# A graph attention layer on one Trainium2 core: all tiles of edges gathered by indirect DMA

## The reference

```python
Qh = (x @ Wq.T + bq).reshape(n, H, D)          # H = 4 heads of D = 16
Kh = (x @ Wk.T + bk).reshape(n, H, D)
Vh = (x @ Wv.T + bv).reshape(n, H, D)
Ee = (edge_attr @ We.T + be).reshape(-1, H, D)
score = (Kh[src] * Qh[dst] * (1.0 / np.sqrt(D)) * Ee).sum(-1)
score = jnp.exp(jnp.clip(score, -5.0, 5.0))
msg = Vh[src] * score[..., None]
wV = jax.ops.segment_sum(msg, dst, num_segments=n)
x = _layernorm(x + wV.reshape(n, H * D), axis=-1)
```

## Time and profile before

| | us |
|---|---|
| median of three timed runs | 1892.74 (1892.62 to 1893.34) |
| span of the profiled execution | 2801.3 |
| POOL busy in it | 1400.8 (50%) |
| TensorE busy in it | 1925.7 (69%) |
| VectorE busy in it | 1174.3 (42%) |
| ScalarE busy in it | 851.7 (30%) |
| mean granted clock of TensorE, as a share of 2.4 GHz | 0.771 |

### The profile page before, as it was taken

How to read it: one execution, slowest core, us unless ns; L and a number is a source line. 1 busy time by engine, 2 the same in 40 slices (tenths; PEclk the granted TensorE clock), 3 DMA queues, 4 the chain that set the end, 5 groups by cost and what they waited for, 6 DMA issues and landing times. The chain is left out here.

```text
span 2801.3 us, 49920 instructions
## 1 busy us (share of the span) xinstructions
PE 1925.7 (69%) x16647; PEld 1663.0 (59%) x16647; DVE 1174.3 (42%) x2092; ACT 851.7 (30%) x2863; POOL 1400.8 (50%) x1495
## 2 busy tenths in 40 slices
PE   4666677777767667776767676667676667766775
PEld 4555666666656556665656665656565656655665
DVE  4433444444434444444444444434344444434444
ACT  6222222332223223223322222223232223222233
POOL 5444554455554445555445555445545545555443
PEclk7777777777778777787877877778778777778776
DMA  6222222222222222222222222222222222222221
GB/s 194 63 56 57 59 58 58 57 61 57 58 54 59 56 58 60 58 59 59 59 57 58 59 57 58 57 56 60 57 58 58 59 57 60 59 58 59 56 61 45
DMA packets 113024, 171.42 MB, mean 61 GB/s; under 512 B 59952, under 2 KB 60592, under 8 KB 112880
## 3 DMA queue, kind: packets, MB, share of 16 engines
q0 software_dynamic: 46848, 96.04, 13.5%
q1 hardware_dynamic: 66160, 75.18, 9.8%
HBM read 163.85 MB, written 7.23 MB: 61 GB/s over the span
## 5 line engine op out<-in xcount | busy, mean ns | idle before, releaser
L275 POOL DMA_INDIRECT kv<-kv_table,idx x1464 | 1384.4, 946 | 1351.1 <-DVE idx L303 944.9
L675 PE MATMUL xg_bank<-x_parts,src_onehot 128*128 128x192 bf16 x7252 | 904.6, 286 | 102.7 <-issue 99.1
L675 PEld LDWEIGHTS xg_bank<-x_parts,src_onehot 128*128 128x128 bf16 x7252 | 739.8, 115 | 187.4 <-issue 129.2
L803 DVE TENSOR_TENSOR src_onehot<-src_ps,columns 128x1664 bf16<-128x1664 bf16 (+1 forms) x592 | 573.0, 968 | 537.0 <-remote 359.3
L646 PE MATMUL qe_ps<-q_win,onehot_t 128*128 128x128 bf16 x2418 | 250.2, 267 | 407.2 <-issue 389.9
L646 PEld LDWEIGHTS qe_ps<-q_win,onehot_t 128*128 128x128 bf16 x2418 | 194.3, 120 | 441.2 <-issue 439.5
L735 ACT COPY onehot_t<-oht_bank 128x512 bf16<-128x512 bf16 x202 | 118.0, 584 | 1099.3 <-remote 1052.4
L743 ACT ACTIVATE distance<-iota_w,dst_neg 128x64 f32<-128x64 f32 x1612 | 405.9, 337 | 15.4 <-PEq L306 15.4
L656 PE MATMUL sum_ps<-onehot,msg 128*64 128x64 f32 x3224 | 357.7, 290 | 49.3 <-issue 42.4
L656 PEld LDWEIGHTS sum_ps<-onehot,msg 128*64 128x64 f32 x3224 | 319.8, 200 | 111.1 <-issue 93.8
L844 DVE TENSOR_TENSOR msg<-kv,sum_ps 128x512 f32<-128x512 f32 x202 | 138.0, 683 | 563.2 <-ACT sum_ps L772 497.0
(11 more groups left out here) (117 smaller groups left out, 760.9 us busy)
## 6 DMA issues: line engine op xcount, KB each, us to landing
attr_sb<-attr SPq DMA_DIRECT2D x201, 256.0 KB
kv<-kv_table,idx POOLq DMA_INDIRECT x1464
q_win<-q_table SPq DMA_DIRECT2D x404, 24.0 KB
kv_table<-kv_stage SPq DMA_DIRECT2D x7, 448.0 KB, 3.6
q_table<-q_stage SPq DMA_DIRECT2D x7, 336.0 KB
xT_sb<-xT SPq DMA_DIRECT2D x7, 224.0 KB, 4.8
kv_stage<-x_own_rows SPq DMA_DIRECT2D x1, 1568.0 KB
out<-y_sb SPq DMA_DIRECT2D x5, 256.0 KB, 2.0
```

The costliest lines, as they stand in the source:

```text
L275: pool.indirect_dma_start(out=kv[:, slot, t, :], out_offset=None, in_=kv_table, in_offset=bass.IndirectOffsetOnAxis(ap=idx[:, slot, t:t + ...
L675: mm = pe.matmul(xg_ps[k % 2], src_onehot[:, c, :], x_parts[:, c, :, :], start=(c == 0), stop=(c == NT - 1))
L803: dve.tensor_tensor(src_onehot[:, PARTS[part], :], src_ps.unsqueeze(1).to_broadcast([P, n, P]), columns[:, PARTS[part], :], ALU.is_equal). ...
```

## The change

All 1612 tiles are gathered by POOL's indirect DMAs. All that served the 148 tiles on TensorE goes: `x_parts`, `columns`, `src_f`, `minus_first`, `src_seen`, `src_onehot`, `xg_sb`, `xg_t_sb`, the second load of x, nine semaphores of the loop and the schedule. VectorE's wait before line 824 counts eight tiles a turn. The two PSUM banks stay as spare banks for setup and end; the freed PSUM bank of `src_ps` isn't used.

```diff
@@ counts and waits @@
-        def gathered_before(slot, turn):
-            if isinstance(turn, int) and turn == 0:
-                return 0
-            if slot == 2:
-                return turn * T
-            return turn * (T - 1) + (1 if slot < 2 else 0)
-        def pool_tiles(g, slot):
-            return T - 1 if pe_tile(g, slot) else 2 * pairs_of(g)
         def gather(pool, g, slot, first=0, end=T):
-            for t in range(first, min(end, pool_tiles(g, slot))):
+            for t in range(first, min(end, 2 * pairs_of(g))):
                 pool.indirect_dma_start(
...
@@ setup @@
-                sp.dma_start(x_own, x_own_rows).then_inc(x_own_loaded, 16)
                 sp.dma_start(src_sb[:, SLOTS * T:], src_tab[:, SLOTS * T:]).then_inc(src_loaded, 16)
...
-                pool.iota(column_i[:, :], ...).then_inc(column_set, 1)
-                pool.wait_ge(column_set, 1)
-                pool.memset(xg_t_sb[:, :], 1.0).then_inc(consts_zeroed, 1)
-                pool.iota(minus_first_i[:, :], ...).then_inc(iota_set, 1)
...
-                number_columns(HALVES[0])
...
-                act.wait_ge(x_own_loaded, 16)
-                for half in HALVES:
-                    act.copy(x_parts[:, half, 0, :], x_own[:, half, :]).then_inc(x_part0, 1)
-                for n, half in enumerate(HALVES):
-                    act.wait_ge(x_rested, n + 1)
-                    act.copy(x_parts[:, half, 1, :], x_rest[:, half, :]).then_inc(x_part1, 1)
-                act.wait_ge(src_loaded, 32)
-                act.copy(src_f[:, :], src_sb[:, :])
-                number_columns(HALVES[1])
...
-                dve.tensor_copy(minus_first[:, :], minus_first_i[:, :]).then_inc(dst_step, 1)
...
-                for n, half in enumerate(HALVES):
-                    dve.wait_ge(x_part0, n + 1)
-                    dve.tensor_tensor(x_rest[:, half, :], x_own[:, half, :], x_parts[:, half, 0, :], ALU.subtract)
-                for n, half in enumerate(HALVES):
-                    dve.wait_ge(x_part1, n + 1)
-                    dve.tensor_tensor(x_parts[:, half, 2, :], x_rest[:, half, :], x_parts[:, half, 1, :], ALU.subtract)
-                dve.wait_ge(x_part2, 2)
@@ loop, TensorE @@
                     def step(g, i, j):
-                        parts, done, turned = parts_at(i, j), done_at(i, j), turned_at(i, j)
                         ... edges_and_onehot(g + 1, ...)
-                        if done is not None:
-                            turn_x(done, DONE_AT[j] % 3)
-                        for part in parts[0:early][0:1]:
-                            gather_part(*part)
-                        if turned is not None and j < 3:
-                            turn_sources(turned)
                         ... fetch_q(g + 1, ...)
-                        if done is not None:
-                            project(done, DONE_AT[j] % 3)
-                        for part in parts[0:early][1:2]:
-                            gather_part(*part)
                         sum_messages(g, j)
-                        for part in parts[early:]:
-                            gather_part(*part)
-                        if turned is not None and j == 3:
-                            turn_sources(turned)
@@ loop, ScalarE @@
-                            act.copy(xg_sb[:, :, :], xg_ps[k % 2]).then_inc(x_kept, 1)
-                            act.copy(xg_t_sb[0:F, :], xg_t_ps[k % 2]).then_inc(x_turned_kept, 1)
-                            act.copy(kv[:, (j + 1) % SLOTS, T - 1, :], xg_kv_ps[k % 2]).then_inc(pe_kv_made, 1)
-                            see_sources(*seen)
@@ loop, VectorE @@
-                        dve.wait_ge(kv_gathered[slot], 16 * (gathered_before(slot, i) + pool_tiles(g, slot)))
-                        if pe_tile(g, slot):
-                            dve.wait_ge(pe_kv_made, i * 3 + (-1, 0, None, 1)[slot])
+                        dve.wait_ge(kv_gathered[slot], 16 * (i * T + n))
...
-                        for part in parts[0:1]:
-                            make_src_onehot(*part)
-                        for part in parts[1:2]:
-                            make_src_onehot(*part)
-                        for part in parts[2:3]:
-                            make_src_onehot(*part)
```

More of the change, by code:

```diff
@@ L66, with gnn_kernel @@
 assert CHUNKS * CH == NT and PASSES * W == NPAD and N < NPAD
[L68 to L73, removed]
 assert ITERS * SLOTS < G <= GPAD and TILES % 2 == 0 and SLOTS == 4
-def gnn_kernel(nc, xT, x_own_rows, w_kvq, We_t, be_row, src_tab, dst_tab, dst_first, attr, out):
+def gnn_kernel(nc, xT, w_kvq, We_t, be_row, src_tab, dst_tab, dst_first, attr, out):
     ctx = ExitStack()
@@ L139, in gnn_kernel @@
         iota_i = sb("iota_i", [P, W], I32, first)
-        column_i = sb("column_i", [P, NT], I32, first)
-        minus_first_i = sb("minus_first_i", [P, P], I32, first)
         ee_ps = [ps(f"ee_ps{i}", [P, T, F], F32) for i in range(2)]
         qe_ps = ps("qe_ps", [P, T, F], F32)
-        xg_banks = [ps(f"xg_bank{i}", [P, 4, P], F32) for i in range(2)]
+        spare_banks = [ps(f"spare_bank{i}", [P, 4, P], F32) for i in range(2)]
         oht_bank = ps("oht_bank", [P, PAIRS, P], F32)
@@ L278, in gather @@
                     .then_inc(kv_gathered[slot], 16)
-        def is_tile(q):
-            return not isinstance(q, int) or 0 <= q < PE_TILES
-        def parts_at(i, j):
-            return [(i * 3 + k, k, part) for k, part in PARTS_AT[j] if is_tile(i * 3 + k)]
-        def done_at(i, j):
-            return i * 3 + DONE_AT[j] if DONE_AT[j] is not None and is_tile(i * 3 + DONE_AT[j]) else None
-        def turned_at(i, j):
-            return i * 3 + j if j >= 1 and is_tile(i * 3 + j) else None
-        def seen_at(i, j):
-            if j == 3 or not is_tile(i * 3 + (j + 1)):
-                return None
-            return i * 3 + (j + 1), i * SLOTS + (SLOTS + j + j // 2)
         def copy_indices(dve, g, slot):
@@ L414, in _ @@
             def _(act):
-                def number_columns(cols):
-                    n = cols.stop - cols.start
-                    act.copy(columns[:, cols, :], column_i[:, cols].unsqueeze(2).to_broadcast([P, n, P]))
                 act.wait_ge(zero_set, 1)
                 act.activation(zero_exp[:, :], zero[:, :], ACT.Exp)
-                act.wait_ge(column_set, 1)
-                number_columns(HALVES[0])
                 for c in range(CHUNKS):
@@ L540, in _ @@
                    .then_inc(dst_step, 1)
[L541 removed]
+                dve.wait_ge(dst_step, 7)
                 dve.tensor_scalar(base_i[:, :], base_f[:, :], one_pass[:, :], None, ALU.mult).then_inc(dst_step, 1)
@@ L658, in sum_messages @@
                         mm.then_inc(sums_made, 1)
-                    def turn_sources(q):
-                        pe.wait_ge(src_seen_made, q + 1)
-                        if not (isinstance(q, int) and q == 0):
-                            pe.wait_ge(src_onehot_made, q * 4)
-                        pe.transpose(src_ps, src_seen[:, :], ident_b[:, :]).then_inc(src_turned, 1)
-                    def gather_part(q, k, part):
-                        if part == 0:
-                            before = q + (0, -2, -1)[k]
-                            if not (isinstance(before, int) and before <= 0):
-                                pe.wait_ge(pe_kv_made, before)
-                        pe.wait_ge(src_onehot_made, q * 4 + (part + 1))
-                        for c in range(PARTS[part].start, PARTS[part].stop):
-                            mm = pe.matmul(xg_ps[k % 2], src_onehot[:, c, :], x_parts[:, c, :, :],
-                                           start=(c == 0), stop=(c == NT - 1))
-                        mm.then_inc(x_gathered, 1)
@@ L795, in _ @@
                 def _(dve):
-                    def make_src_onehot(q, k, part):
-                        n = PARTS[part].stop - PARTS[part].start
-                        if part == 0:
-                            dve.wait_ge(src_turned, q + 1)
-                        if not (isinstance(q, int) and q == 0):
-                            dve.wait_ge(x_gathered, q * 4 + (part - 3))
-                        dve.tensor_tensor(src_onehot[:, PARTS[part], :], src_ps.unsqueeze(1).to_broadcast([P, n, P]),
-                                          columns[:, PARTS[part], :], ALU.is_equal).then_inc(src_onehot_made, 1)
                     def add_sums(g, slot):
```

89 lines of the change are left out of this document (11 added, 78 removed).

## The result

The changed kernel takes 2076.93 us (median of four runs, 2076.06 to 2080.35) where the kernel before, run beside it, takes 1892.68 (1892.25 to 1893.34): a ratio of 1.098, interval 1.096 to 1.099. The forecast was 2073.5 us; it is 3.4 us short, 1.9% of the 184 us that the change costs.

The account below looks back on a forecast made before the run. The prediction took POOL's 1464 gathers, 1.2485 us each, to bound the kernel: 1892.74 + 184.8 for 148 more gathers - 4.0 for setup = 2073.5 us, +9.6%. Its bounds were 2065 to 2089, the low side widened to 2055.

Parts of the forecast that it names:

- POOL's gathers pace: Main loop: the timed kernel before is bound by POOL's 1464 gathers, 97% of its time; forecast's chance 0.88.
- closing sum: Whole kernel before: start, 1447 gathers at 1.2485 us, landing and end give 1891.8 us against 1892.74 measured.
- Step 1: POOL in the loop: 148 added gathers at 1.2485 us each, all on the path, +184.8 us.
- Step 2: Loop work removed from TensorE, ScalarE and VectorE: none on the path if POOL sets the pace, worth 0.
- the 20 us: Loop: room left before the index copy that frees a slot would make POOL wait, some 20 us.
- Step 3: Setup: removed loads and VectorE passes shorten idleness before the reduction, which starts at 38 to 39 us; -4 us.
- the bounds: Setup gain between nothing and 7.2 us, made of 5.83 us of idleness before the reduction and 1.38 of a long gather.
- Step 4: End of the kernel: only names change, TensorE may arrive at the lower clock; 0, at worst +1 us.
- The stretch: Profile of the kernel before: 908 us of its 2801.3 us span absent from timed runs, taken as a cost of recording.
- Rival 1: Loop: TensorE's stage paces and gathers are cheaper; faster below 1.134 us a gather, down to 1587 us; chance 0.05, slower-by-less 0.03.
- Rival 2: Loop: the removed VectorE comparisons slow POOL's gathers by 0.39 us each, so the change gives 1448 us; chance 0.01.
- Rival 3: Loop: TensorE at low clock with engines in series becomes a new bound, 2671 us, half way 2368; chance 0.03.

Follow-up runs that it names:

- e1: Changed kernel without 148 of its gathers, those tiles gathered by nobody: 1891.34 us against 1892.53 for the kernel before, ratio 0.9994.
- e2: Kernel before with all its tile machinery, plus POOL gathering the 148 tiles into an unread spare tile: 2077.34 us, ratio 1.098.
- e3: Changed kernel with at most four gathers a group, 808 instead of 1612, other rows zero: 1073.43 us, one run.
- e10: Kernel before with the reduction over partitions put ahead of the first gather, at the fast pace: 1887.97 us against 1892.88, ratio 0.9977.
- e7: Kernel before with the reduction over partitions put ahead of the first gather, at the slow pace: 2806.36 us against 2807.73, ratio 0.9988.
- a2: Changed kernel again, unedited, in the fourth job at the slow pace: 2765.24 us against 2884.15 for the kernel before, ratio 0.960.
- e6: Changed kernel with four VectorE copies of 128 x 1024 fp32 added per group: 2680.21 us at the slow pace, no changed kernel run beside it.
- a1: Changed kernel again, unedited, in the third job: 2076.17 us against 1892.88 for the kernel before, ratio 1.097.
- e4: Changed kernel with the reduction over partitions put ahead of the first gather: 2070.42 us against 2076.93 for the changed kernel.

## Why the prediction was right, and where it was not

**POOL's gathers pace: right.** The closing sum held. e1 takes the removed machinery out alone and nothing changes beyond the setup's microsecond; e2 adds the gathers alone and gives the whole loss; a gather is worth 1.249 us in e2 and 1.248 in e3, against the 1.2485 of the earlier trace rows.

**Step 1, +184.8 us: right.** 148 x 1.2483 = 184.7. Between 8 x 1.2485 and the next group no extra is paid: in the whole run the waits for the index copy come to 0.9 us. The +10 us kept in the range for the group changes weren't needed.

**Step 2, worth 0: right.** Room enough was there, since POOL waits 0.9 us in all; how much of the 20 us it was, no run measured.

**Step 3, -4 us: mis-sized.** The loop begins 1.4 us earlier (58.26 against 59.70). What I had put down to a queue or to VectorE, the 5.8 us ahead of the reduction, stayed: 5.83 in the earlier trace rows, 5.79 after. The DMA engines fall silent 4 us sooner (a share of 0.22 in 36 to 38 us and 0 in 38 to 40, where they were full until 40) and VectorE stands idle there, and the reduction didn't care: it starts at 41.10 us, not at 38 to 39. The gain is the long gather of the earlier trace rows: 2.32 us before, 0.95 after at 34.37 us, the 1.4 that the bounds had as their smaller part. Before, it starts at 34.29 us inside VectorE's first pass over x, which ends at 35.80, and ends 0.81 us after it ends; the change takes that pass away. The 2.6 us missing here are most of the miss; 1892.68 + 184.7 - 1.4 = 2076.0, against 2076.93 and 2076.17 measured.

**Step 4, 0 to +1: right.** VectorE begins on the last group's rows at 2055.03 us, and from there to the end are 23.1 us, where the sum had 23.5. From the last gather's start to these rows are 3.04 us; the sum had 1.2485 + 2.0, the 2.0 taken from an output store.

**The stretch: a wrong inference.** "I take these stalls for a cost of being recorded" was the step that failed. e2 and e10 record nearly as many instructions and aren't stretched; in the second and fourth jobs every timed run is slow. The profile of before was one of an execution at the slow pace: its 2801.3 us lie within the timed runs of the second job (2796.34 to 2816.96), and e7 has its waits. The sum came out right because it used the stretches in which POOL waits for nobody, and a gather there is the same at either pace. The check that I had named for the diagnosis, POOL's wait falling below 50 us and the span below 2130, came true (0.9 and 2078.1) and proved nothing: a2 is the same kernel, with a wait of 710.1 us and a span of 2763.6. Halving TensorE's instructions doesn't remove the stretch: at the slow pace the kernel after takes 33% longer (2765.24 / 2076.93), that before 52% (2884.15 / 1892.88).

**The rivals.** Rival 1 is refuted at the fast pace: a gather costs 1.249 us in timed runs, far from its 1.134, and e1 shows that nothing else paces. At the slow pace something of its kind holds: TensorE's side ends the waits, and taking its work away gains 4%. Had the timed runs fallen into such a job, the sign would have been the other one. The forecast left that out, because it had explained the stretch away. Rival 2 is refuted for the comparisons: the distance is 1.2483 us in e1 without them and in e10 with them. But VectorE can shut POOL out. Gathers that start inside line 508, 524, 528 or 544 of the kernel before, which read two or more tensors in SBUF, are held until it ends; the 209 that start well inside a comparison in the profile of before, and those inside lines 824, 830 and 844, where one operand is in PSUM, take 0.94 to 0.95 us. Line 515, as large as line 508 (128x448) but with one operand in PSUM, holds none either. The Trainium skill (SBUF — State Buffer, Who interferes with whom) says that a VectorE copy in a two-port mode blocks the other engine for the whole instruction, and e6's copies do (they pass 1024 elements in 686 ns, while line 600's product passes 512 in as many). It exempts two-tensor operations from that mode, but has those with both inputs in SBUF contend with GpSimd's reads. The forecast left that condition out; the rows here bear it out. Rival 3 didn't occur: TensorE is at the low clock, as its condition had it, with 5.5 us of work in a group where 5.1 to 5.7 were expected, and the engines overlap.

## What to carry to other kernels

If a chain of equal instructions on one engine, at the distance that they keep where nothing holds them, closes the timed run's sum to a microsecond, the price of one more such instruction can be taken from it, and work beside it that doesn't hold the chain costs nothing. But a profile that is far longer than the timed runs may be of another state of the chip, as here, and not a tax of the recorder: ask what the change does in that state as well, and compare only kernels of one job. A reduction over partitions on POOL belongs where POOL waits anyway. Long VectorE operations on two SBUF tensors, and large copies, don't belong beside gathers that are on the path.

## What the runs showed of the hardware

- At the fast pace an indirect gather of 128 rows of 512 bytes costs POOL 1.2483 to 1.2508 us, 0.94 to 0.95 busy and 0.30 to 0.31 before the next, with TensorE busy 55% or 80% and with or without VectorE's comparisons.
- A gather that starts inside a VectorE copy of 128 x 1024 fp32 (e6), or inside a VectorE operation on two SBUF tensors (before, after, e2, e4, e10), ends 0.80 to 0.82 us after that operation: up to 2.52 us in place of 0.94 (e10). VectorE operations with one operand in PSUM leave it at 0.94 to 0.95.
- A reduction over partitions behind eight gathers starts 5.8 to 5.9 us after them (before, after, e1, e2, a1). With no gather ahead it starts 2.8 us (e4) or 2.1 us (e10) after its input is made. Putting it into POOL's wait for the table made the kernel before 4.9 us faster and the kernel after 5.8 to 6.5.
- One kernel on one chip took 1892.88 us in one job and 2884.15 in another, in every run of each. In the slow one TensorE stands still for much of each burst of gathers, and two of its signals are recorded 17 us after their matmuls (a2); the cause is open.
